# Four graph layers on 64 graphs: probability tiles turned by VectorE and scratch DMAs instead of TensorE, split low parts on GpSimd, staged weight loads, new issue orders

## What is computed

```python
def _layernorm(x, axis=-1, eps=1e-5): ...
# layer 0: e = leaky(x W1 (x W2)^T); masked softmax; relu(att @ (x W3))
x = _layernorm(x + _L0_gnn_ref(x, adj, W1, W2, W3))
# layer 1: e = leaky(s1_i + s2_j), s = (x W) a; masked softmax; elu(att @ (x W))
x = _layernorm(x + _L1_gnn_ref(x, adj, W, a))
# layer 2: relu(x mlp1 + b1) -> attention without mask (W_fc, 512 wide) -> elu, residual,
#          relu(. mlp2 + b2) -> masked attention (W_hand) -> elu, residual, relu
x = _layernorm(x + _L2_gnn_ref(x, adj, ...))
# layer 3: four-head masked attention with q, k, v, and the projection wo
x = _layernorm(x + _L3_gnn_ref(x, adj, ...))
```

## Time and profile before

| | |
|---|---|
| device time, 3 runs | median 2921.05 us (2909.83 to 2933.94) |
| the profiled execution | 2918.28 us, of which the span (first to last instruction) is 2916.5 us |
| PE, DVE, ACT, POOL busy | 92%, 78%, 69%, 53% of the span |
| mean granted TensorE clock | 0.983 of full speed |

### The profile page before, as it was taken

One profiled execution on the slowest core, in us unless ns is written; L12 is line 12 of the kernel. 1 busy time (PEld: TensorE's weight loads), 2 busy tenths in 40 slices (PEclk: granted clock), 3 DMA queues, 4 the chain that ended last, 5 costly groups with the idle time before them and its releaser, 6 DMA issues.

```text
span 2916.5 us, 61536 instructions
## 1 busy us (share of the span) xinstructions
PE 2689.4 (92%) x22472; PEld 2551.3 (87%) x22472; DVE 2278.2 (78%) x6124; ACT 1998.7 (69%) x4801; POOL 1556.0 (53%) x2119
## 2 busy tenths in 40 slices
PE   4689999999999999999999999999999999999974
PEld 4589999999999999998999998999999999998863
DVE  3257888888888888888888887888888888888874
ACT  1357777777777776777777777777777777776752
POOL 0235555555555555555556555555655555555542
...
DMA packets 132766, 195.17 MB, mean 67 GB/s; under 512 B 14832, under 2 KB 97136, under 8 KB 132464
## 3 DMA queue, kind: packets, MB, share of 16 engines
...
## 4 chain that ended last, share of the span: by engine, by line
PE 60%; DMA 13%; ACT 8%; SPq 8%; DVE 6%; issue 4%; POOL 1%; POOLq 0%; DVEq 0%
PE ps L224 29%; DMA p4T<-scratch 10%; PE ps L378 6%; SPq L208 6%; PE ps L240 5%; PE ps L436 4%; PE ps L337 4%; PE ps L233 3%; PE ps L338 3%; DMA scratch<-p 3%; DVE p L950 3%; PE ps L456 2%; ACT p L671 2%; PE ps L360 2%; DVE h_lo L692 1%
## 5 line engine op out<-in xcount | busy, mean ns | idle before, releaser
L1067 POOL TENSOR_TENSOR p<-p,rd 128x512 f32<-128x512 f32 x256 | 269.8, 1054 | 20.0
L671 ACT ACTIVATE p<-p,nmx 128x256 f32<-128x256 f32 x512 | 255.7, 504 | 25.4 <-DVE nmx L935 25.2
L991 POOL TENSOR_TENSOR o1Tp_lo<-o1T,o1Tp_hi 128x1024 fp32r<-128x1024 f32 x64 | 153.8, 2403 | 220.8 <-ACT o1Tp_hi L472 220.8
L1003 POOL TENSOR_SCALAR xn<-act,nmean,rstd 128x256 f32<-128x256 f32 x384 | 243.6, 643 | 18.3 <-POOL rstd L998 11.2
L456 PE MATMUL ps<-p4T,v 128*64 128x256 f32 x1024 | 144.3, 404 | 118.2 <-DMA p4T<-scratch 117.7
L995 POOL TENSOR_TENSOR vare<-mv,eps 128x2 f32<-128x2 f32 x256 | 108.0, 422 | 270.5 <-DVE mv L748 270.5
L1060 POOL TENSOR_TENSOR rd<-some,den 128x2 f32<-128x2 f32 x256 | 53.5, 209 | 354.6 <-DVE den L944 354.6
L456 PEld LDWEIGHTS ps<-p4T,v 128*64 128x64 f32 x1024 | 67.3, 140 | 178.1 <-DMA p4T<-scratch 96.5
L692 DVE TENSOR_TENSOR xnT_lo<-ps,xnT_hi 128x512 fp32r<-128x512 f32 x192 | 132.1, 688 | 114.2 <-ACT xnT_hi L472 114.2
L935 DVE CUSTOM_DVE_ANT_0 p<-ps,mask 128x256 f32<-128x256 f32 x512 | 189.9, 418 | 33.3 <-PE ps L436 33.3
L480 ACT ACTIVATE sco<-sco,nmax 128x256 f32<-128x256 f32 x384 | 191.0, 500 | 28.9 <-DVE nmax L736 28.9
...
## 6 DMA issues: line engine op xcount, KB each, us to landing
scratch<-p SPq DMA_DIRECT2D x128, 512.0 KB, 2.9
p4T<-scratch SPq DMA_DIRECT2D x512, 128.0 KB, 3.9
...
o1T<-in_mlp SPq DMA_DIRECT2D x1, 512.0 KB, 4.4
p<-in_mlp SPq DMA_DIRECT2D x1, 512.0 KB, 4.5
att<-in_fc SPq DMA_DIRECT2D x1, 512.0 KB, 5.4
```

The costliest lines, as they stand in the source:

```text
L671: ins = nc.scalar.activation(rows_, rows_, ACT.Exp, scale=-1.0, bias=nmx4[:, h, m:m + 1], accum_out=den4[:, h, m:m + 1])
L991: return G.tensor_tensor(lo, whole, hi.bitcast(fp32), ALU.subtract)
L1003: ins = G.tensor_scalar(xn[:, m, :], y[:, m, :], nmean[i][:, m:m + 1], rstd[i][:, m:m + 1], ALU.add, ALU.mult)
L1067: G.tensor_tensor(rows_, rows_, rd4[:, h, :].unsqueeze(2).unsqueeze(3).broadcast_to([P, NT, QUADS, CT * QP]), ALU.mult).then_inc(S["p4n"], 1)
```

## The change

- The PE steps `t0`, `t1`, `t3` (transposes of `sco`) and `o3` (transposes of `o3T`) are gone. In their place `t0`, `t1`, `t3` on DVE transpose the 32x32 blocks of `sco` (128x512) into `act`; SP writes `act` to scratch (`pro_out`) and reads it back into `sco` by four DMAs (`pro_in`); ACT takes the high part from `sco`, and POOL, in three new steps, the low part. `o3T` goes the same way, through `sco2` into a new tile `o3r`, and `r3` adds it from SBUF in two pieces.
- New waits follow from shared tiles: `t` on DVE waits for the previous graph's `xn`, `e` for the previous `proT`, `a` on ACT for the scratch write.
- `n4` moves from DVE to POOL. `xb4` is gone: the bias is added in place in `xn2` after its transposes. `xn3` is one tile. `xnT0` and `xnT1` are one pair; `x0T` shares the memory of `x0Tp`'s low part, `pfc` that of `pfcp`'s; `o4T` is its own pair, and the leaky scores of the unmasked layer go to `pfc` in SBUF, not to bank 5.
- PSUM banks are handed on by `enter`, which waits for the last step that reads the bank. `n3` on PE is merged in `m3`. The layers' banks are partly other ones.
- Weights load in four groups; the first graph needs only the first (`W1T`, `W2T`, `W3`). The rest of the setup is put ahead of the first use of each weight, inside the orders (`before` of `run`).
- All five orders are other ones.

```diff
-    "sp": "lt:0 o40:7 st:9 o42:7 lx:1 i40:7 i42:7",
+    "sp": "o42:8 i40:8 i42:8 st:9 o1:3 o5:6 lx:1 o0:1 lt:0 i1:3 i0:1 o3:6 i5:6 i3:6 o40:7",
+    "pe": "x0:4 v4:9 b2:7 n2:6 s40:9 v2:7 w2:7 s42:9 a1:5 h1:4 g0:2 c2:6 a0:3 a3:8 f1:4 r2:6 h0:2 m3:7 s0:2 x1:5 a4:9 f2:6 x3:8 m2:5 y4:9 h3:7 q4:8 k4:8 f3:7 d2:6",
...
+            def pro_out(i):
+                def step(t):
+                    sp.wait_ge(S[f"pro{i}_x"], t + 1)
+                    wait(sp, S[f"pro{i}_dma"], back(t - 1))
+                    sp.dma_start(scratch_pro[i].rearrange("p w n -> p (w n)"), flat(act[i])).then_inc(S[f"pro{i}_dma"], 16)
+            def pro_in(i):
+                def step(t):
+                    sp.wait_ge(S[f"pro{i}_dma"], sent(t))
...
+                    for w in range(QUADS):
+                        sp.dma_start(rows_[w * QP:(w + 1) * QP, :, :], scratch_pro[i][:, w, :].rearrange("(q j) n -> j q n", q=QUADS)).then_inc(S[f"pro{i}_dma"], 16)
...
-            def t3(t):
-                pe.wait_ge(S["pro2"], t + 1)
-                transposes(bank[3], sco[2]).then_inc(S["proT2_mm"], 1)
...
             def t3(t):
-                dv.wait_ge(S["proT2h"], t + 1)
-                low_part(proT[2], bank[3]).then_inc(S["proT2"], 1)
+                dv.wait_ge(S["pro2"], t + 1)
+                wait(dv, S["xn2"], t)
+                turn(2).then_inc(S["pro2_x"], 1)
...
             def r3(t):
-                dv.wait_ge(S["on3_mm"], t + 1)
+                dv.wait_ge(S["o3_dma"], back(t))
                 dv.wait_ge(S["q3"], t + 1)
-                V.tensor_tensor(act[2][:, :, :], act[2][:, :, :], bank[2], ALU.add).then_inc(S["r3"], 1)
+                for m in range(NT):
+                    row = act[2][:, m, :].rearrange("p (k q c) -> p k q c", k=CT, q=QUADS)
+                    ins = V.tensor_tensor(row, row, o3r[:, :, :, m, :].rearrange("p q k c -> p k q c"), ALU.add)
+                ins.then_inc(S["r3"], 1)
...
+            def t3(t):
+                po.wait_ge(S["proT2h"], t + 1)
+                low_of_turned(proT[2], 2).then_inc(S["proT2"], 1)
```

More of the change, by code:

```diff
@@ L18, in parse, with run @@
     return [(name, int(stage)) for name, stage in (x.split(":") for x in text.split())]
-def run(engine, steps, B):
+def run(engine, steps, B, before={}):
     order = parse(ORDERS[engine])
@@ L27, in run @@
             if 0 <= k - s < B:
+                if k == s and name in before:
+                    before[name]()
                 steps[name](k - s)
@@ L105, in graph_stack @@
         lrow = sb("lrow", [P, N])
-        pfc = sb("pfc", [P, NT, N])
-        pfcp = parts("pfcp", [P, NT, N])
+        *pfcp, pfc = parts_in_place("pfcp", [P, NT, N])
         rdc = sb("rdc", [P, NT])
@@ L371, in w2 @@
             def w2(t):
-                pe.wait_ge(S["rdb"], t + 1)
-                product3(bank[5], hfc, pfcp, NT, 2, off=2).then_inc(S["w2_mm"], 1)
-            def mlp2(m):
-                for k in range(HT):
-                    for i, (a, b) in enumerate(PAIRS):
-                        ins = nc.tensor.matmul(bank[3][:, m, :], WP["mlp2"][a][:, k, m * P:(m + 1) * P], o2T[b][:, k, :],
-                                               start=(k == 0 and i == 0), stop=(k == HT - 1 and i == 2))
-                return ins
+                pe.wait_ge(S["pfcl"], t + 1)
@@ L648, in x3_ @@
                 ac.wait_ge(S["xnT2_mm"], t + 1)
+                wait(ac, S["q4_mm"], t)
                 wait(ac, S["k4_mm"], t)
@@ L725, in _ @@
[L725 to L731 removed]
+            dv.wait_ge(S["setup_dve"], 1)
@@ L864, in z2, with o3 @@
                 low_part(o2T, att[:, :, :]).then_inc(S["o2T"], 1)
+            def o3(t):
+                dv.wait_ge(S["o3T"], t + 1)
+                wait(dv, S["proT2"], t)
+                blocks = o3T[:, :, :].rearrange("p k n -> p (k n)").rearrange("p (c w j) -> p w c j", w=QUADS, j=QP)
+                V.transpose(sco[2][:, :, :, :].rearrange("p b a n -> p (b a n)").rearrange("p (w c j) -> p w c j", w=QUADS, j=QP), blocks).then_inc(S["o3_x"], 1)
             def h3_(t):
                 dv.wait_ge(S["h3h"], t + 1)
+                wait(dv, S["raw2"], t)
                 V.tensor_copy(cols[3][:, :, :], ps[:, 2:4, C:C2])
```

529 lines of the change are left out of this document (322 added, 207 removed), and 7 rows, old and new, of the table ORDERS.

## The result

| | before | changed |
|---|---|---|
| device time, 4 runs each | median 2924.36 us (2909.83 to 2933.94) | median 2781.44 us (2776.03 to 2789.57) |
| ratio | | 0.9515, 95% interval 0.9476 to 0.9554 |
| the profiled execution, its span | 2918.28, 2916.5 us | 2789.57, 2787.8 us |
| one period: store to store, mean of 50 | 42.62 us (546.36 to 2677.25) | 40.56 us (485.69 to 2513.62) |

The kernel is faster by 4.85%; the prediction said 2754 us, 5.7%. The period is within 0.1 us of the predicted 40.5. What is missing lies mostly at the end of the run.

The account below looks back on a forecast made before the run. The prediction took PE to bound the kernel: 39.2 us of work plus 0.5 + 0.5 + 0.3 of waits, a 40.5 us period. 2916.5 - 64 x 2.2 - 24 = 2752, plus 1.8, gave 2754 us; range 2685 to 2860 (8 in 10).

Parts of the forecast that it names:

- The term of the four sets: On PE, four sets of transposes go: 0.44 + 0.44 + 0.44 + 0.36 and 0.2 for switches, 1.9 us a period.
- as a rule of such a fit: At `a4`'s second half, 28.6 against 29.0 us on paper, yet a PE wait of 0.5 us was taken.
- the second half of `a4`: PE's use of the turned `s42`: was to wait 0.5 us a period, before 1.5.
- The chain to `x3`: From `a3` to the norm: 12.0 to 12.4 us against 11.8 of PE work, so PE waits 0.5 us.
- Rival 3: Layer 2's turn reaches `a3` 2 us late: period 42.0 us, 2849 us in all; chance 0.13.
- 0.1 to 0.5 us ahead of `a3`: Layer 2's turn: POOL done by 16.7 to 17.1 us, `a3` starts at 17.2; covered, but just.
- Rival 2: POOL and DVE block each other at SBUF; `r3`, norm, low part grow up to 0.5 us; period 41.3, 2804 us; chance 0.20.
- The start: Staged weight loads: first product at about 14 us, 31 earlier; net 24 us earlier, bounds 5 and 35.
- 64 x 2.2: All 64 periods were each to get 2.2 us shorter, from 42.7 to 40.5 us.
- with the three longer turns of the first graph: In the fill, part of the 7 us of later setup taken as seen, off the start's gain.

Follow-up runs that it names:

- e4: The changed kernel with four sets of four fp32 transposes that nothing waits for put back on PE; 2805.41 us, 0.9659 of the kernel before.
- e5: The kernel before with each of the four removed sets of transposes issued twice; 2974.52 us, 1.0214 of the kernel before.
- e8: The changed kernel with the four reads of layer 2's turn split into eight; 2781.17 us, 0.9556 of the kernel before.
- e2: The changed kernel with layer 2's turn moved ahead of the last head on POOL and of `k2` on ScalarE; 2754.09 us, 0.9476 of the kernel before.
- e3_both: The changed kernel with the move of e2, and `l0` behind `p3` on ScalarE; 2743.57 us, 0.9436 of the kernel before.
- e12: The changed kernel with `l0` behind `p3`, and layer 2's turn ahead of three heads on POOL and earlier on ScalarE; 2767.77 us, 0.9508 of the kernel before.

## Why the prediction was right, and where it was off

**The bound and the period: right, partly by luck in the split.** Predicted 40.5, measured 40.56. The sum was 39.2 of PE and 1.3 of waits; the runs give 39.0 (e4) to 39.4 (e5: 41.06 - 1.66) of PE, and 1.2 to 1.5 of waits. The term of the four sets was 1.9 us, with 0.2 for switches; measured 1.66, so the 0.2 isn't there. The step that predicted waits "as a rule of such a fit" was the important one: it is what e4 and e5 confirm, since 1.7 us of PE work moved the period by 0.2 us in the changed kernel and by 0.8 in the one before. The size of these waits was a guess that came out, not a sum. And the prediction gave the 2.2 us to the work taken off PE, with the holes nearly as large as before (1.3 against 1.6 us). The sum comes out, but e4, with that work put back, loses only 0.2 us of it: the orders and chains had room for a PE list of 40.7 us, which the prediction had no term for.

**Where the waits stand: half right.** `a3` was to cost part of 0.3 us and costs 0.5, `x1` costs 0.2; `x3` and the second half of `a4`, which were to wait 0.5 each, show no wait in full passes. The chain to `x3` was worked out with `c3` and `z3` at their lengths before. Both got shorter: `c3` from a mean of 894 ns (L885) to 408 (L1033), and `z3` from a mean of 1096 ns (L902, median 1050 in the earlier trace rows) to 695 in L1053. Together that is 0.9 us, more than the 0.2 to 0.6 us that PE was to wait. The first row below is `z3` now; the second belongs to the durations further down.

```profile
L1053 DVE SCALAR_TENSOR_TENSOR act<-act,xn 128x512 f32<-128x512 f32 x64 | 44.5, 695 | 0.1
L865 DVE STREAM_TRANSPOSE act<-sco 128x512 f32<-128x512 f32 x192 | 133.2, 694 | 57.2 <-ACT sco L555 56.3
```

**Rival 3, the turn of layer 2: the right place, a quarter of the size, another mechanism.** The fit of "0.1 to 0.5 us ahead of `a3`" was that tight; it fell 0.5 us short on average, not for SP or the DMA engines (e8) but for what stands ahead of it in the orders of ScalarE (`k2`) and POOL (the four heads), as e2 shows for both together. The sum had no room for the heads: it put POOL right behind ScalarE. In the period shown POOL is done at 1249.63, and PE, ready 1.18 us before, starts at 1249.68.

**Rival 2, the contested port: present, elsewhere, not shown to set the period.** The lines grew by 0.7 us each on average, but `n2`, `i2`, `j2` and not `r3` or the norm; P = 41.3 did not come. The rule that I cited from the Trainium skill, page "SBUF — State Buffer", section "SBUF: two separate sides", has a second half that I left out: it names a DVE operation in a two-port mode beside one with two SBUF inputs as what locks the pair against GpSimd. L989 reads one SBUF tile only, and doubled from 673 to 1400 ns; in the period shown it starts 0.2 us after a POOL multiplication that lasts 1.10. That L989 runs in a two-port mode is not seen in a trace, but its 668 ns, where the two-input lines of the same size take 1225 to 1231 unblocked (L984, and L998 in `e3_both`), fit it. With that, the trace agrees with the whole rule.

**Durations.** The new transposes last 694 ns; I had 0.62, half of 1230: too little by 0.07. POOL's low parts of 128x512 are 1.27 to 1.30, the lower bound of the earlier trace rows. POOL 30.7 us a period (predicted 29.4 to 31.3), ACT 30.7 (31), DVE 35.8 (34.6; the three blocked lines add 2.06, and `c3` and `z3` take 0.9 off), DMA share 0.41 (0.5). The reads of 64 KB land after 2.4 us where I used 3.9 to 5.0 of the 128 KB reads, which is why the transfer had more room than my sum said. The Trainium skill, page "DMA: Bandwidth & Descriptors", section "Anatomy of one DMA — SWDGE (gpsimd) path", gives a fixed cost of about 2.0 us, fitted to DMAs issued from GpSimd. Those here are issued by SP; with 2.1 and 2.4 us for reads of 64 KB they come near it.

**The start: right.** First product at 14.11 us (predicted about 14), 31.05 us earlier (predicted 31); the first load of x 27.3 us earlier, where the sum took 24 net of what the later setup costs in the fill.

**The step that failed: "64 x 2.2", with nothing outside the full passes but the start.** The sum gave all 64 periods the gain of a full pass and added the start. Only 55 are full; they gained 112 us (sum: 121). The other nine, which fill and drain, were to gain 20 and lost 10.5. That is 30 of the 36 us by which the profiled execution misses 2754, nearly all of it in the drain (27.7; the fill 2.6); 9 come from the 55 passes, and the start gave 3 back. In the drain PE idles 12.9 us more, at a clock of 0.87 in place of 0.92, and its largest wait is for the new turn (27.9 us, where before it was 30.8 for the heads' transfer, now 15.0): there each graph's chain through its steps counts, and PE's shorter list does not. That is read from the waits; which chain makes up the whole loss stays open, since cutting that wait to 9.0 us (e12) left the drain at 260.0. My term "with the three longer turns of the first graph" saw this for the fill and not for the drain.
